# Sums of weight blocks: from GpSimd's adds to accumulating DMA transfers

## The reference

```python
qkv = silu(x @ qkv_w.T)                      # 32 heads x (q, k, v) x 128
scores = (q @ k.T) * decay(head, distance)   # the reference goes block by block
attn = scores @ v
normed = norm_w * attn * rsqrt(mean(attn * attn) + eps)
x = layernorm(x + (sigmoid(x @ gate_w.T) * normed) @ out_w.T)
x = layernorm(x + x @ base_W.T + base_b + lora(x))
```

## The kernel before

| unit | 0 | 1 | 2 | 3 | 4 | 5 | 6 | 7 |
|---|---|---|---|---|---|---|---|---|
| holds at the end | b11 | b11+b12 | b11+b12+b22 | b21 | b22+b12 | b22 | b11+b12+b22+b21 | no operand |

## Time and profile before

### The profile page before, as it was taken

One profiled execution on the slowest core, in us unless ns is written; L12 is line 12 of the kernel. 1 busy time (PEld: TensorE's weight loads), 2 busy tenths in 40 slices (PEclk: granted clock), 3 DMA queues, 4 the chain that ended last, 5 costly groups with the idle time before them and its releaser, 6 DMA issues.

```text
span 1014.2 us, 15712 instructions
## 1 busy us (share of the span) xinstructions
PE 1000.2 (99%) x5620; PEld 874.8 (86%) x5620; DVE 780.2 (77%) x1102; ACT 664.7 (66%) x1108; POOL 350.0 (35%) x329
## 2 busy tenths in 40 slices
PE   9999999999999999999999999999999999999996
PEld 7888988889888898889988898888978899888886
DVE  6777975887857976779757879579777797699885
ACT  6577754777467764677647774677637786477644
POOL 1353232341443223433323414342234323331462
PEclk9999999999999999999999999999999999999999
DMA  6021111110211111211111112111112111110402
GB/s 202 27 63 51 50 47 55 56 47 28 68 42 47 48 55 41 62 48 53 47 56 55 39 35 68 42 47 48 47 48 63 35 65 48 42 48 22 146 22 83
DMA packets 48814, 55.67 MB, mean 55 GB/s; under 512 B 4321, under 2 KB 40033, under 8 KB 48737
## 3 DMA queue, kind: packets, MB, share of 16 engines
q1 hardware_dynamic: 48736, 54.67, 17.0%
HBM read 52.56 MB, written 2.10 MB: 54 GB/s over the span
## 4 chain that ended last, share of the span: by engine, by line
PE 87%; DVE 6%; issue 2%; ACT 2%; POOL 1%; DMA 1%; SPq 0%; POOLq 0%; DVEq 0%; ACTq 0%
PE ps L1833 20%; PE ps L1834 19%; PE ps L1835 19%; PE ps L1827 9%; PE ps L1828 8%; PE ps L1829 8%; PE ps L1940 1%; PE ps L1925 1%; DVE wl L1048 1%; PE ps L1942 1%; DVE s L1029 1%; PE ps L1927 1%; ACT wh L387 1%; DVE yl L1029 1%; DVE acc L1148 1%
## 5 line engine op out<-in xcount | busy, mean ns | idle before, releaser
L1833 PE MATMUL ps<-xh,wh 128*128 128x512 f32 x658 | 261.8, 398 | 0.6 <-ACT stg L435 0.6
L1834 PE MATMUL ps<-xl,wh 128*128 128x512 f32 x658 | 257.2, 391 | 0.0
L1835 PE MATMUL ps<-xh,wl 128*128 128x512 f32 x658 | 256.1, 389 | 0.0
L1742 POOL TENSOR_TENSOR stage<-stage 128x512 f32<-128x512 f32 x61 | 87.4, 1432 | 331.4 <-DMA stage<-stream 331.3
L1762 POOL TENSOR_TENSOR sqacc<-sqacc,sq 128x512 f32<-128x512 f32 x64 | 92.3, 1442 | 271.1 <-ACT sq L546 271.1
L1029 DVE TENSOR_TENSOR wl<-stage,wh 128x1024 fp32r<-128x1024 f32 (+2 forms) x145 | 159.4, 1109 | 32.1 <-ACT wh L387 32.1
L387 ACT ACTIVATE wh<-stage 128x1024 fp32r<-128x1024 f32 (+2 forms) x145 | 122.1, 855 | 53.8 <-PE ps L1829 33.7
L1835 PEld LDWEIGHTS ps<-xh,wl 128*128 128x128 f32 x658 | 123.6, 188 | 26.6
L1833 PEld LDWEIGHTS ps<-xh,wh 128*128 128x128 f32 x658 | 123.5, 188 | 24.0 <-issue 1.0
L1834 PEld LDWEIGHTS ps<-xl,wh 128*128 128x128 f32 x658 | 123.9, 188 | 22.0
L1833 PE MATMUL ps<-wh,xh 128*128 128x256 f32 (+1 forms) x416 | 121.1, 291 | 0.0
(11 more groups left out here) (201 smaller groups left out, 2220.5 us busy)
## 6 DMA issues: line engine op xcount, KB each, us to landing
stage<-stream SPq DMA_DIRECT2D x61, 384.0 KB, 3.3
stage<-stream SPq DMA_DIRECT2D x42, 256.0 KB, 2.8
stage<-stream SPq DMA_DIRECT2D x63, 128.0 KB, 2.1
dec<-decay SPq DMA_DIRECT2D x32, 128.0 KB, 2.0
acc<-xt SPq DMA_DIRECT2D x8, 256.0 KB, 5.7
v<-x SPq DMA_DIRECT2D x8, 256.0 KB, 4.9
out<-acc SPq DMA_DIRECT2D x8, 256.0 KB, 2.1
sfull<-lora_router SPq DMA_DIRECT2D x1, 512.0 KB, 6.0
```

Of the source, the lines that this page charges most:

```text
L1742: nc.gpsimd.tensor_tensor(stage[:, s, 1:5:3, :], stage[:, s, 0:6:5, :], stage[:, s, 7:8, :].broadcast_to([P, 2, U]), ALU.add).then_inc(t_p ...
L1833: nc.tensor.matmul(dst, wt[0], mv_[0], start=start, stop=False, skip_group_check=True)
L1834: nc.tensor.matmul(dst, wt[0], mv_[1], start=False, stop=False, skip_group_check=True)
L1835: return nc.tensor.matmul(dst, wt[1], mv_[0], start=False, stop=stop, skip_group_check=True)
```

## The change

The host makes the block loads twice as long and adds a second array, `addends`. A block is now loaded with all eight units filled (1 MB): b11, b11, b11, b21, b12, b22, b11, b22. SP still issues it as two transfers, of four units each (512 KB), L305 and L306. For each block `addends` holds five pieces: b12, b22, b12, b12, b21.

POOL makes no addition for the sums. It issues three DMA transfers that add what they bring to what is there: three pieces from `addends` onto units 2, 4 and 6 (384 KB), two pieces onto units 1 and 7 (256 KB), then, when both have landed (`t_part`), units 5 and 7 onto units 2 and 6, from the stage to the stage (256 KB). So unit 7 holds b22+b21 when it is added to b11+b12 in unit 6. `t_sum` counts 16 for each block, and ACT waits for that. Loads without sums (`oa`, `ob`, first and last ones) have the same bytes as before; in `stream` they are padded with zeros that are not loaded.

```diff
-                sp.dma_start(stage[:, s, 0, :], stream[m, :, 0, :]).then_inc(t_in[s], 16)
-                sp.dma_start(stage[:, s, 3:8:2, :], stream[m, :, 1:4, :]).then_inc(t_in[s], 16)
+                sp.dma_start(stage[:, s, 0:4, :], stream[m, :, 0:4, :]).then_inc(t_in[s], 16)
+                sp.dma_start(stage[:, s, 4:8, :], stream[m, :, 4:8, :]).then_inc(t_in[s], 16)
...
-                act.wait_ge(t_sum, block_no(g, [...].index(name)) + 1)
+                act.wait_ge(t_sum, 16 * block_no(g, [...].index(name)) + 16)
...
             def sums(g, name):
 
                 m = load_no(g, name)
+                n = block_no(g, ["qk0", "va", "vb", "g01", "qk1", "g23", "qk2", "qk3"].index(name))
                 s = m % 2
                 pool.wait_ge(t_in[s], 32 * ((m + 1) // 2))
-                nc.gpsimd.tensor_tensor(stage[:, s, 1:5:3, :], stage[:, s, 0:6:5, :],
-                                        stage[:, s, 7:8, :].broadcast_to([P, 2, U]), ALU.add).then_inc(t_part, 1)
-                pool.wait_ge(t_part, parts[0] + 1)
-                nc.gpsimd.tensor_tensor(stage[:, s, 2, :], stage[:, s, 1, :], stage[:, s, 5, :], ALU.add)\
-                    .then_inc(t_part, 1)
-                pool.wait_ge(t_part, parts[0] + 2)
-                parts[0] += 2
-                nc.gpsimd.tensor_tensor(stage[:, s, 6, :], stage[:, s, 2, :], stage[:, s, 3, :], ALU.add)\
-                    .then_inc(t_sum, 1)
+                nc.gpsimd.dma_start(stage[:, s, 2:8:2, :], addends[n, :, 0:3, :], accum_op=ALU.add).then_inc(t_part, 16)
+                nc.gpsimd.dma_start(stage[:, s, 1:8:6, :], addends[n, :, 3:5, :], accum_op=ALU.add).then_inc(t_part, 16)
+                pool.wait_ge(t_part, 32 * n + 32)
+                nc.gpsimd.dma_start(stage[:, s, 2:7:4, :], stage[:, s, 5:8:2, :], accum_op=ALU.add).then_inc(t_sum, 16)
...
+    addends = []
+
+    def units(b11, b21, b12, b22):
+
+        addends.append(np.stack([b12, b22, b12, b12, b21], axis=1))
+        return np.stack([b11, b11, b11, b21, b12, b22, b11, b22], axis=1)
```

More of the change, by code:

```diff
@@ L90, in heads_before, with build @@
     return HG * group_of(n) + sum(b < place_of(n) for b in (QK0, QK1, QK2, QK3))
-def build(nc, stream, xt, x, decay, norm_w, base_b, lora_router, router_b, expert_map, ident_in, ones_in, fresh_in, out):
+def build(nc, stream, addends, xt, x, decay, norm_w, base_b, lora_router, router_b, expert_map, ident_in, ones_in, fresh_in, out):
     ctx = ExitStack()
@@ L391, in sums_hi @@
                 m = load_no(g, name)
-                act.wait_ge(t_sum, block_no(g, ["qk0", "va", "vb", "g01", "qk1", "g23", "qk2", "qk3"].index(name)) + 1)
+                act.wait_ge(t_sum, 16 * block_no(g, ["qk0", "va", "vb", "g01", "qk1", "g23", "qk2", "qk3"].index(name)) + 16)
                 wait_free(act, g, name, part)
@@ L1733, in add_bias @@
                 nc.gpsimd.tensor_tensor(acc[:, t, :], acc[:, t, :], bb, ALU.add).then_inc(bias_added, 1)
-            parts = [0]
             def sums(g, name):
                 m = load_no(g, name)
+                n = block_no(g, ["qk0", "va", "vb", "g01", "qk1", "g23", "qk2", "qk3"].index(name))
                 s = m % 2
                 pool.wait_ge(t_in[s], 32 * ((m + 1) // 2))
-                nc.gpsimd.tensor_tensor(stage[:, s, 1:5:3, :], stage[:, s, 0:6:5, :],
-                                        stage[:, s, 7:8, :].broadcast_to([P, 2, U]), ALU.add).then_inc(t_part, 1)
-                pool.wait_ge(t_part, parts[0] + 1)
-                nc.gpsimd.tensor_tensor(stage[:, s, 2, :], stage[:, s, 1, :], stage[:, s, 5, :], ALU.add)\
-                    .then_inc(t_part, 1)
-                pool.wait_ge(t_part, parts[0] + 2)
-                parts[0] += 2
-                nc.gpsimd.tensor_tensor(stage[:, s, 6, :], stage[:, s, 2, :], stage[:, s, 3, :], ALU.add)\
-                    .then_inc(t_sum, 1)
+                nc.gpsimd.dma_start(stage[:, s, 2:8:2, :], addends[n, :, 0:3, :], accum_op=ALU.add).then_inc(t_part, 16)
+                nc.gpsimd.dma_start(stage[:, s, 1:8:6, :], addends[n, :, 3:5, :], accum_op=ALU.add).then_inc(t_part, 16)
+                pool.wait_ge(t_part, 32 * n + 32)
+                nc.gpsimd.dma_start(stage[:, s, 2:7:4, :], stage[:, s, 5:8:2, :], accum_op=ALU.add).then_inc(t_sum, 16)
             def next_sums(g, name):
@@ L2326, in halves @@
         return [w[:, 2 * i:2 * i + 2, :].transpose(2, 1, 0).reshape(P, U) for i in range(2)]
+    addends = []
+    def units(b11, b21, b12, b22):
+        addends.append(np.stack([b12, b22, b12, b12, b21], axis=1))
+        return np.stack([b11, b11, b11, b21, b12, b22, b11, b22], axis=1)
     def paired(w1, w2):
-        (b11, b21), (b12, b22) = halves(w1), halves(w2)
-        return np.stack([b11, b21, b22, b12], axis=1)
+        return units(*halves(w1), *halves(w2))
     def value_block(g, k):
@@ L2334, in value_block @@
         b = [[w[j, :, 2 * i + k, :].T for j in range(2)] for i in range(2)]
-        return np.stack([b[0][0], b[1][0], b[1][1], b[0][1]], axis=1)
+        return units(b[0][0], b[1][0], b[0][1], b[1][1])
     def rows(a, b):
-        return np.concatenate([a.reshape(P, 2, U), b.reshape(P, 2, U)], axis=1)
+        return np.concatenate([a.reshape(P, 2, U), b.reshape(P, 2, U), np.zeros((P, 4, U), np.float32)], axis=1)
     blocks = []
@@ L2347 @@
                 (q0, q1), (k0, k1) = halves(qkv[h, 0]), halves(qkv[h, 1])
-                blocks.append(np.stack([q0, k0, q1, k1], axis=1))
+                blocks.append(rows(np.stack([q0, k0], axis=1), np.stack([q1, k1], axis=1)))
             elif name[:5] == "first":
@@ L2382 @@
     arrays = {
-        "stream": np.stack(blocks), "xt": xt, "x": x, "decay": decay_tables(),
+        "stream": np.stack(blocks), "addends": np.stack(addends), "xt": xt, "x": x, "decay": decay_tables(),
         "norm_w": np.asarray(L0_attn_norm_w).reshape(HEADS, P).T,
```

## The result

| | before | after |
|---|---|---|
| median, us | 1015.26 | 1425.66 (4 runs, 1420.86 to 1429.88) |
| profiled execution / its span, us | 1015.99 / 1014.2 | 1422.18 / 1420.4 |
| PE busy / PE idle, us | 1000.2 / 14.0 | 1105.1 / 315.3 |
| DVE, ACT, POOL busy, us | 780.2, 664.7, 350.0 | 745.4, 661.9, 352.8 |
| mean granted clock | 1.00 | 0.88 |

The ratio is 1.4033, 95% interval 1.4005 to 1.4062. The kernel is slower, as forecast, but the time lies 261 us above the forecast and outside the range. Of the 406 us that the span grew, 301 are idle time of PE and 105 are matmuls that run longer.

The account below looks back on a forecast made before the run. PE, busy 1000.2 of 1014.2 us, was taken as the bound; 1016 plus 132 of stalls plus 21 for first and last groups less 3 for DVE gave 1166, so a 1165 us median; range 1035 to 1330.

Parts of the forecast that it names:

- The load: SP's block load, doubled to 1 MB in two transfers, was to take 4.9 us instead of 3.5.
- The undisturbed sum: POOL's three adding transfers per block: 7.0 us for the pair, 4.4 for the third, 11.4 instead of 3.6.
- The four places: First copies of `g01`, `qk2`, next `qk0` and `vb`, bearing 9.2, 11.1, 12.2, 13.1 us of L; stalls 132 us.
- the account: PE's stalls summed from how far L exceeds each place's room: 132 us, plus 21 for first and last groups.
- L: Time from issue of a block's load to its sums being ready: 7.1 us before, 16.3 forecast.
- DVE's relief: DVE's 128x768 subtraction, freed of POOL's adds, was to drop towards 0.96 us; taken as 3 us gained.
- Cheap transfers: Rival: each adding transfer costs what a plain one does, L 11.8 us and time 1038 us; chance 0.20.
- Slow additions: Rival: adding packets run at a quarter of a plain one's rate, L 21.9 us, time 1344 us; chance 0.12.
- The other blocks: `qk1`, `g23`, `qk3` and `va` were costed at nothing, their cover gone only if L passes some 20 us.
- POOL's queue: Additions of squares behind each block's third issue: costed at nothing; if uncovered, 1.3 us in each of 7 groups.
- The line of 32 us for each us of L: Whole kernel: each us of L worth about 32 us, from 27 places and 5 in the first and last groups.
- The third rival: TensorE's clock falls in each of seven `g01` stalls, adding some 30 us: 1195 us; chance 0.12.

Follow-up runs that it names:

- run 2: Kernel before with only the changed kernel's 1 MB loads, POOL still making the sums with its three adds: 1019.10 us, ratio 1.0044.
- run 8: Changed kernel with a 4096-byte descriptor area, and SP's block load also waiting for the sums of the block before: 1335.83 us, ratio 1.3154.
- run 6: Kernel before with eleven fills of a spare area on POOL ahead of each block's three adds, delaying the sums: 1205.58 us, ratio 1.1871.
- run 1: Changed kernel with 4096 instead of 1024 bytes per SBUF partition for descriptors of GpSimd-issued transfers: 1313.35 us, ratio 1.2942.
- run 7: Changed kernel with a 4096-byte descriptor area and the three transfers copying instead of adding: 1182.48 us, ratio 1.1644.
- run 13: Kernel before with 16 fills on POOL ahead of each block's additions, no addition done by DMA: 1376.74 us, ratio 1.3565.
- run 10: Changed kernel with a 4096-byte descriptor area and the third transfer replaced by one addition on POOL: 1199.38 us, ratio 1.1796.
- run 14: Kernel before with eleven POOL fills per block, plus 25 unused matmuls ahead of output tile 2's wait for `y`: 1190.88 us, ratio 1.1735.
- run 11: Changed kernel with 53 unused matmuls on PE ahead of output tile 2's wait for `y` in seven groups: 1438.79 us, ratio 1.4132.
- run 12: Changed kernel with a 4096-byte descriptor area, POOL issuing the pairs of `qk3` and `va` ahead of the additions of squares: 1302.55 us, ratio 1.2811.
- run 9: Changed kernel, descriptor area left at 1024 bytes, with the three transfers copying instead of adding: 1189.78 us, ratio 1.1702.
- run 3: Kernel before with the first of POOL's adds done four times in each block: 1129.82 us.
- run 5: Kernel before with five fills of an unread area on POOL for each block: 1049.74 us, ratio 1.0337.

## Why the prediction was wrong

**Right.** The direction and the floor: PE stood at 99%, and nothing was to be won. The load, 4.9 us (median 4.8 to 5.3 where nothing disturbs it; run 2 shows it harmless). The undisturbed sum, 11.4 (run 8: 11.0), with its parts: the pair 7.0 (7.2) and the third 4.4 (3.8, to its landing); nothing had shown an adding transfer, so the factor of two for its bytes was a guess that came near. The four places and what each bears (run 6: 128 us of idle time by the account and by the trace; run 1: 241 and 227 with the L measured there; in the changed kernel `g01` waits 97.5 us, and 14.1 x 7 is 99). DVE's relief to 956 ns a subtraction; it was worth nothing, since DVE waits too. "Cheap transfers" was a rival against which run 7 speaks: even plain copies give 1182 us. "Slow additions" gave 1344, nearest to the result, but its mechanism is not what happened: an undisturbed addition runs at the forecast price.

**Wrong.** Two terms of the sum failed. L came out at 20.4 to 24.0 us at the four places instead of 16.3 (mean 22.6), and the matmuls' own time, which was to stay unchanged, grew by 105 us. Step by step:

1. *"two at once (384 and 256 KB)."* The second issue came 5.4 us after the first, in `g01` 9.3, once the first had landed, for want of room in the descriptor area. POOL's own issue time of 1.3 us was weighed as a price; that an issue can wait was not among the bounds. For the same want of room the first issue of `qk1`, `g23`, `qk2` and `qk0` waits until the block before has landed whole. Worth 112 us (run 1).
2. *"It goes from 512 KB in two transfers to 1 MB in two, still two issues on SP, so nothing more is queued there."* Nothing waits on SP, but the next block's load now runs beside the sum of this one: the 384 KB transfer takes 9.0 instead of 5.2 us in `g01`, 8.1 in `qk2` (run 8 against run 1). The range had bounds for bytes and rate, none for sharing. What it is worth in time no run shows by itself, since keeping the load apart puts it in the chain; an estimate follows below.
3. *"The other blocks have more: ... I cost them at nothing; that cover is gone only if L passes some 20 us"*, and *"POOL's queue: I cost it at nothing of its own."* These are one error. POOL issues in order and waits for the pair between its issues, so each block holds it from its first issue to its third: 7 to 10.6 us in run 1, 10.3 to 14.2 in the changed kernel, where an addition of its own had held it for 3.6. `qk1`, `g23`, `qk3` and `va` start 5 to 12 us after their data are there (`g23` for want of room, point 1), L there is 26 to 34 us (past the limit that the prediction named, as at the four places), and but for `qk1` ACT waits 5.5 to 7.3 us at each. PE's waits behind these blocks are 91 us in the changed kernel and 17 in run 1. Run 13 shows that lateness and an occupied POOL alone make 1377 us. The line of 32 us for each us of L is not what failed: it is 30 from run 6 to run 13, 33 from run 10 to run 1 and 33 from run 1 to the changed kernel, the clock's share included. That it held is in part luck, since in PE's idle time alone it is 23, 27 and 22. What failed is one L for all places: once POOL is still taken when a load lands, L grows by more than the sum does.
4. *The third rival*, the clock, was the right mechanism at too few places: 4 us for each of 7 stalls in `g01`, 30 us. At L = 15.5 it falls 30 times and adds 62 us to PE's busy time (run 6); half the falls are worth 25 us of that and 15 of the end time (run 14). In the changed kernel the records have 46 stretches at the lower level, 333 us of them, and PE is busy 105 us longer. How much of this the end time would give back stays open, since run 11 took hardly any of it away.

In figures, from 1165 to 1426 us: 112 are the wait for room. The other 149, from 1165 to run 1's 1313, are in its profile 77 us of PE's idle time beyond the forecast (227 against 132 + 21 - 3 = 150) and 72 us by which its matmuls run longer. In run 1 POOL begins within 0.5 us of the load's landing at the four places, and L passes 16.3 there since the sums take 12.6 to 14.5 us instead of 11.4; undisturbed they take 11.0. So the 77 are, by the account, mostly the price of loads beside sums. That is worked out and not measured by itself. POOL's order has a small part in them: run 12 took 11 us back by order alone.

## What to carry to other kernels

Time a chain of transfers by when its engine is free again, not only by when its data land: an engine that issues in order and waits between issues is occupied for the whole chain. Once that comes near the time between blocks, places with room of their own stall as well, and a block's lateness is passed on to the next (here 4 us more of POOL for each block made two of them 7 us later). Before moving work into accumulating transfers, see that several of them fit into the descriptor area at once, and what load will run beside them. And where PE is at 99% with small margins, price each stall with the clock that falls behind it (here 2 us of longer matmuls for each of the 30 stalls of run 6).

## What the runs showed of the hardware that was not expected

- With a descriptor area of 1024 bytes the second adding transfer's issue waited 5.4 us for the first (384 KB) to land, and the next block's first issue for the third; the profile names both waits only "issue". At 4096 bytes the second issue followed after 0.8 us. Copies of the same shapes fitted into 1024 bytes (runs 1, 9).
- An adding transfer took 5.2 us for 384 KB from memory and 3.8 for 256 KB within the chip, a plain one 3.7 and 2.5; POOL's issue took 1.2 to 1.3 us against 0.7 to 0.8 (runs 7, 8). In the mean a packet of the adding ones had 972 bytes and took 107 ns, one of the copies 3374 bytes and 160 ns (changed kernel, run 7).
- Beside one 1 MB load the adding transfer of 384 KB took 9.0 us, a copying one 6.2 (runs 1, 7).
- POOL's additions slow DVE and its fills don't: the subtraction of 128x768 took 1267 ns in the mean with repeated additions and 956 with fills (runs 3, 5), and the two kernels lie 80 us apart, where their L differs by 1.3 us in the mean of the four places, worth some 42.
- The clock fell once at each of the 30 stalls of run 6; in the changed kernel PE was busy for 0.39 of the 14 us from 369 to 383, and the 6 us behind them ran at 0.50.
